# Attention probabilities read back from DRAM in four transfers by row block instead of four by partition block

## The chip, the cores and the metric

The kernel runs on one core of a Trainium2 chip. The metric is the device time of one execution in microseconds (us). The core has a matrix engine (TensorE, PE in the profile), a vector engine (VectorE, DVE), a scalar engine (ScalarE, ACT), GpSimd (POOL), and a sync engine (SyncE, SP), whose queue issues every transfer of this kernel. The transfers run on the core's 16 DMA engines.

## The reference

Eight batches of 112 tokens (width 1024) pass through two layers. Each layer has a cross attention against a context of 375 rows for each batch, and a low-rank mixture of experts. The change touches the second attention, which has 32 query heads in 8 groups of 4 (a group shares one key and one value head of width 128):

```python
q = apply_rope(query @ wq)          # 32 heads
k = apply_rope(key @ wk)            # 8 heads, each used by 4 query heads
scores = einsum('bhqd,bhkd->bhqk', q, k) / sqrt(128)
attn = softmax(scores + mask)
out = einsum('bhqk,bhkd->bhqd', attn, v)
return out.reshape(bs, sq, HQ * DV) @ wo
```

## The kernel before, in words

All arithmetic is float32. A product is made of three passes over operands split into a high and a low part: ScalarE rounds the high part, GpSimd or VectorE subtracts to get the low part.

The second attention is a pipeline of 64 steps, one for each pair of key group g and batch u (s = 8 g + u). `attention_phase` writes the order of each engine's queue out by hand. For one step s the work is: four score products (queries by keys, `scores`), mask and row minimum (`mask_scores`, L1696), exponentials (`exps`, L1704), normalisation, transposition of the probabilities, the product with the values (three key tiles, `o_banks`), and the projection with `wo` (`project`, 24 products a step).

The transposition is done in two parts. VectorE turns blocks of 32 by 32 inside groups of 32 partitions (`transpose`, L1739) and leaves them in `in_blocks[:, t]`, which has 128 partitions with 4 blocks of 384 numbers. Then the blocks must change partitions, and this goes through a DRAM tensor, `p_dram`, of shape (2, 128, 4, 384):

- `carry_out` (L1750) writes all of `in_blocks[:, t]` to `p_dram[t]` in one transfer of 768 KB.
- `carry_in` (L1761) waits until that transfer has landed (semaphore `carried`), and reads the data back into `pt_raw[t]` (the profile calls the two buffers `e_shuffled_then_xn_t` and `e_shuffled`) in four transfers of 192 KB. Row 32 i + a, block j of `p_dram[t]` goes to partition 32 j + a, place i. Every contiguous piece is 384 numbers, 1536 bytes, in both memories.

When all four have landed (semaphore `shuffled[t]` at a multiple of 64), ScalarE takes the high part of `pt_raw` (L1928), VectorE and GpSimd the low part (L1993, L1950), and TensorE multiplies with the values.

In step s the SP queue issues, in this order: `carry_out(s + 2)`, the queries and keys of step s + 6 (L1632, L1634), the values of step s + 2 (L1639), `carry_in(s + 2)`, and one or two tiles of `wo` (L1886). The queue is in order: while it waits in front of one transfer, the later ones are not issued. `carry_out(s + 2)` waits for the transposes of step s + 2, which VectorE does in step s. The second pair of these transposes comes behind VectorE's own part of the split of step s's probabilities (`probabilities_low(s)`), and so behind the landing of `carry_in(s)`. The carries of steps 0 and 1 are issued earlier, in `query1_phase`, between the last query projections.

Of the kernel before, what the change touches and what calls it, by code (L numbers as in the profile page):

```python
# [37 lines left out]
BLOCK, BLOCKS = 32, 4  # L38
# [1547 lines left out]
class AttentionSteps:  # L1586
# [165 lines left out]
    def carry_in(self, sp, s):  # L1752


        t = s % 2
        sp.wait_ge(self.carried, 16 * s + 16)
        if s >= 2:
            sp.wait_ge(self.pt_low_first, s - 1)
            sp.wait_ge(self.pt_low, 2 * s - 2)
        for j in range(BLOCKS):  # L1760
            sp.dma_start(self.pt_raw[t][BLOCK * j:BLOCK * (j + 1)],  # L1761
                         self.k.p_dram[t, :, j].rearrange("(i a) x -> a i x", i=BLOCKS)).then_inc(
                self.shuffled[t], 16)

    def load_mask(self, sp):
        sp.dma_start(self.mask, self.k.mask).then_inc(self.mask_in, 16)
# [676 lines left out]
```

## Time and profile before

| | us |
|---|---|
| median of 3 runs | 1777.59 |
| lowest, highest run | 1765.16, 1779.57 |
| the profiled execution: its own time | 1777.91 |
| the profiled execution: span, first to last instruction | 1776.1 |
| PE busy in the span | 1739.9 (98%) |
| transfers out to `p_dram`, x64, each | 768 KB, 6.4 from issue to landing |
| transfers back, x256, each | 192 KB, 3.8 or 3.9 from issue to landing |

The granted clock of TensorE was 1.00 for the core. A row of the profile's page is a share of the span or of one of 40 equal slices of it; the attention steps lie between 1137 and 1700 us.

### The profile page before, as it was taken

How to read it: one execution, taken by the hardware profiler on the slowest of the kernel's cores; microseconds unless marked ns; L12 is line 12 of the kernel's file. 1: busy time of each engine (PE TensorE's matmuls, PEld its weight loads, DVE VectorE, ACT ScalarE, POOL GpSimd, SP SyncE). 2: the span in 40 equal slices, each digit the busy share in tenths (PEclk: the TensorE clock that was granted, in tenths of full speed). 3: DMA queues.
4: the chain of work that ended last, by engine and by line, in shares of the span. 5: the costliest groups of instructions: out<-in, count | busy, mean ns of one | idle time of the engine just before them, and what ended most of it. 6: DMA issues, size and time to landing. Idle time of an engine off the chain costs nothing.

```text
span 1776.1 us, 26431 instructions
## 1 busy us (share of the span) xinstructions
PE 1739.9 (98%) x8904; PEld 1576.3 (89%) x8904; DVE 1102.9 (62%) x2116; ACT 735.6 (41%) x1532; POOL 783.0 (44%) x588
## 2 busy tenths in 40 slices
PE   7999999999999999999999999999999999999998
PEld 6999999999888888888999999889989999999876
DVE  7631275566433333336666668898888988888845
ACT  5211210012333233222111023487788888878724
POOL 3223522125422222201222234487777787777724
PEclk9999999999999999999999999999999999999999
DMA  4112342235643333423433335799999999899843
GB/s 135 66 51 83 133 132 85 84 104 162 206 128 121 114 111 117 127 82 99 127 108 89 111 108 163 203 291 265 263 286 278 286 264 276 268 274 278 243 134 111
DMA packets 186402, 291.55 MB, mean 164 GB/s; under 512 B 48336, under 2 KB 146896, under 8 KB 185280
## 3 DMA queue, kind: packets, MB, share of 16 engines
q1 hardware_dynamic: 186304, 290.33, 54.6%
q8 instruction: 51, 0.84, 0.2%
q14 instruction: 47, 0.39, 0.1%
HBM read 193.01 MB, written 97.26 MB: 163 GB/s over the span
## 4 chain that ended last, share of the span: by engine, by line
PE 56%; DMA 20%; SPq 6%; DVE 3%; issue 2%; ACT 1%; POOL 1%; DVEq 0%; ACTq 0%; POOLq 0%
PE bank L200 52%; DMA probabilities<-q_rotated_then_x_rows 17%; SPq L1761 4%; SPq L1886 1%; PE bank L106 1%; PE bank L2328 1%; PE bank L186 1%; PE bank L2341 1%; DVE e_scores L1696 1%; POOL shared_operand_low L324 1%; DMA aw_weights_then_ctx_rows<-in_wk 0%; DVE q_rotated_then_x_rows L1739 0%; DVE e_p_t_low L1993 0%; DMA e_raw_then_a<-q_rotated 0%; POOL w_rest_low L789 0%
## 5 line engine op out<-in xcount | busy, mean ns | idle before, releaser
L200 PE MATMUL bank<-shared_operand_high,w_first_high 128*128 128x448 f32 (+1 forms) x768 | 279.1, 363 | 1.6 <-DVEq L805 0.7
L200 PE MATMUL bank<-shared_operand_low,w_first_high 128*128 128x448 f32 (+1 forms) x768 | 278.4, 363 | 0.0
L200 PE MATMUL bank<-shared_operand_high,w_first_low 128*128 128x448 f32 (+1 forms) x768 | 278.3, 362 | 0.0
L324 POOL TENSOR_TENSOR shared_operand_low<-ctx_raw,shared_operand_high 128x768 fp32r<-128x768 f32 x64 | 119.4, 1877 | 197.4 <-ACT shared_operand_high L320 197.3
L1452 POOL TENSOR_TENSOR w_first_low<-aw_weights_then_ctx_rows,w_first_high 128x1024 fp32r<-128x1024 f32 x30 | 72.1, 2402 | 221.7 <-ACT w_first_high L1420 221.7
L1704 ACT ACTIVATE e_scores<-e_scores,e_least 128x375 f32<-128x375 f32 x256 | 152.5, 597 | 18.7 <-DVE e_least L1696 17.9
L200 PEld LDWEIGHTS bank<-shared_operand_high,w_first_high 128*128 128x128 f32 x768 | 144.7, 188 | 13.2 <-POOL w_first_low L496 1.0
L200 PEld LDWEIGHTS bank<-shared_operand_high,w_first_low 128*128 128x128 f32 x768 | 144.6, 188 | 11.4
L200 PEld LDWEIGHTS bank<-shared_operand_low,w_first_high 128*128 128x128 f32 x768 | 144.7, 188 | 11.1
L320 ACT ACTIVATE shared_operand_high<-ctx_raw 128x768 fp32r<-128x768 f32 x64 | 52.8, 843 | 209.4 <-DMA ctx_raw<-in_ctx_t 190.9
L1696 DVE CUSTOM_DVE_ANT_0 e_scores<-bank,e_mask_then_layer_ffn 128x375 f32<-128x375 f32 x256 | 134.6, 528 | 0.0
L1739 DVE STREAM_TRANSPOSE q_rotated_then_x_rows<-e_scores 128x768 f32<-128x768 f32 x128 | 124.2, 971 | 10.8 <-issue 8.4
L200 PE MATMUL bank<-shared_operand_high,w_rest_high 128*128 128x376 f32 x384 | 128.9, 336 | 1.6 <-POOL w_rest_low L789 1.6
L1420 ACT ACTIVATE w_first_high<-aw_weights_then_ctx_rows 128x1024 fp32r<-128x1024 f32 x30 | 31.8, 1061 | 236.8 <-PE bank L200 195.5
L200 PE MATMUL bank<-shared_operand_high,w_rest_low 128*128 128x376 f32 x384 | 128.6, 335 | 0.0
L200 PE MATMUL bank<-shared_operand_low,w_rest_high 128*128 128x376 f32 x384 | 128.6, 335 | 0.0
L200 PE MATMUL bank<-w_rest_high,shared_operand_high 128*128 128x512 f32 x288 | 112.9, 392 | 0.0
L200 PE MATMUL bank<-w_rest_high,shared_operand_low 128*128 128x512 f32 x288 | 112.4, 390 | 0.0
L200 PE MATMUL bank<-w_rest_low,shared_operand_high 128*128 128x512 f32 x288 | 112.2, 390 | 0.0
L1950 POOL TENSOR_TENSOR e_p_t_low<-e_shuffled_then_xn_t,e_p_t_high 128x448 fp32r<-128x448 f32 x64 | 83.1, 1321 | 56.2 <-ACT e_p_t_high L1928 56.2
L1950 POOL TENSOR_TENSOR e_p_t_low<-e_shuffled,e_p_t_high 128x448 fp32r<-128x448 f32 x64 | 83.1, 1318 | 52.5 <-ACT e_p_t_high L1928 52.5
L1717 DVE TENSOR_SCALAR e_scores<-e_scores,e_inv 128x375 f32<-128x375 f32 x128 | 99.7, 780 | 2.3
(259 smaller groups left out, 4542.8 us busy)
## 6 DMA issues: line engine op xcount, KB each, us to landing
probabilities<-q_rotated_then_x_rows SPq DMA_DIRECT2D x64, 768.0 KB, 6.4
ctx_raw<-in_ctx_t SPq DMA_DIRECT2D x64, 384.0 KB, 3.9
e_shuffled_then_xn_t<-probabilities SPq DMA_DIRECT2D x128, 192.0 KB, 3.8
e_shuffled<-probabilities SPq DMA_DIRECT2D x128, 192.0 KB, 3.9
e_raw_wo<-in_wo SPq DMA_DIRECT2D x64, 256.0 KB, 5.1
aw_weights_then_ctx_rows<-in_wq SPq DMA_DIRECT2D x30, 512.0 KB, 3.8
q_rotated<-q_rotated_then_x_rows SPq DMA_DIRECT2D x64, 224.0 KB, 2.3
e_raw_then_a<-q_rotated SPq DMA_DIRECT2D x64, 224.0 KB, 6.6
```

Source lines behind the costliest of these rows:

```text
L106: last = pe.transpose(banks[j][:, c * SEQ:(c + 1) * SEQ], buf.xn[:, k, ch * P:(ch + 1) * P], ident[0:SEQ, 0:SEQ])
L200: mm = pe.matmul(out, stationary[a], moving[b], start=(first and i == 0), stop=(last and i == 2))
L320: act.activation(k.ctx_ring[0][slot][:, 2 * j:2 * j + 2, :], k.c_raw[:, j % 2], ACT.Copy).then_inc(done, 1)
L324: pool.tensor_tensor(k.ctx_ring[1][slot][:, 2 * j:2 * j + 2, :], k.c_raw[:, j % 2], f32(k.ctx_ring[0][slot][:, 2 * j:2 * j + 2, :]), ALU.s ...
L1420: act.activation(k.w_first[0][:, t], k.raw[:, t], ACT.Copy).then_inc(w_high, 1)
L1452: pool.tensor_tensor(k.w_first[1][:, t], k.raw[:, t], f32(k.w_first[0][:, t]), ALU.subtract).then_inc(w_low, 1)
L1696: dve.tensor_tensor_reduce(self.s_buf[:, t, h, 0:KEYS], self.s_bank[h][:, 0:KEYS], self.mask[:, u, :], 1.0, HIGHEST, ALU.add, ALU.min, sel ...
L1704: act.activation(self.s_buf[:, t, h, 0:KEYS], self.s_buf[:, t, h, 0:KEYS], ACT.Exp, bias=self.least[:, t, h:h + 1], scale=-1.0, accum_out= ...
L1717: dve.tensor_scalar(self.s_buf[:, t, h, 0:KEYS], self.s_buf[:, t, h, 0:KEYS], self.inv[:, t, h:h + 1], None, ALU.mult).then_inc(self.norme ...
L1739: dve.transpose(self.in_blocks[:, t, :, h * piece:(h + 2) * piece].rearrange("p j (m k) -> p m j k", k=BLOCK), self.s_buf[:, t, h:h + 2, : ...
L1761: sp.dma_start(self.pt_raw[t][BLOCK * j:BLOCK * (j + 1)], self.k.p_dram[t, :, j].rearrange("(i a) x -> a i x", i=BLOCKS)).then_inc(self.sh ...
L1950: pool.tensor_tensor(by_block(pt[1][:, c, :]), raw_p(s, c), by_block(f32(pt[0][:, c, :])), ALU.subtract).then_inc(pt_low, 1)
```

## The change

The four transfers of `carry_in` are cut along the other axis. Before, transfer j filled the 32 partitions of block j with all four places i. After, transfer i fills place i of all 128 partitions. The number of transfers, the bytes of each, the 1536-byte pieces, the waits, the semaphores and the order on the queue are the same.

```diff
--- before.py
+++ after.py
@@ -1757,10 +1757,9 @@
         if s >= 2:
             sp.wait_ge(self.pt_low_first, s - 1)
             sp.wait_ge(self.pt_low, 2 * s - 2)
-        for j in range(BLOCKS):
-            sp.dma_start(self.pt_raw[t][BLOCK * j:BLOCK * (j + 1)],
-                         self.k.p_dram[t, :, j].rearrange("(i a) x -> a i x", i=BLOCKS)).then_inc(
-                self.shuffled[t], 16)
+        for i in range(BLOCKS):
+            sp.dma_start(self.pt_raw[t][:, i], self.k.p_dram[t, BLOCK * i:BLOCK * (i + 1)].rearrange(
+                "a j x -> j a x")).then_inc(self.shuffled[t], 16)
```

The access pattern of the source, from the slowest dimension to the fastest, was 32 rows, 4 places, 384 numbers; it becomes 4 blocks, 32 rows, 384 numbers. The destination was 32 partitions of 4 by 384 numbers; it becomes 128 partitions of 384 numbers.

## Rows read from the trace of the kernel before

**Rows 1.** The page: busy TensorE, and the span in 40 slices.
```profile
PE 1739.9 (98%) x8904; PEld 1576.3 (89%) x8904; DVE 1102.9 (62%) x2116; ACT 735.6 (41%) x1532; POOL 783.0 (44%) x588
...
PEclk9999999999999999999999999999999999999999
DMA  4112342235643333423433335799999999899843
GB/s 135 66 51 83 133 132 85 84 104 162 206 128 121 114 111 117 127 82 99 127 108 89 111 108 163 203 291 265 263 286 278 286 264 276 268 274 278 243 134 111
```

**Rows 2.** The chain that ended last, 1400 to 1480 us: shares by line.
```profile
by line: DMA probabilities<-q_rotated_then_x_rows 82.0%; SPq L1761 18.4%; SPq L1886 4.8%; issue 3.4%; SPq L1749 0.2%
```

**Rows 3.** Timeline of the SP queue, one step: start us, us, line, transfer, count.
```profile
1450.63 1.75 SPq L1761 DMA_DIRECT2D e_shuffled_then_xn_t<-probabilities  x4
1452.43 0.43 SPq L1886 DMA_DIRECT2D e_raw_wo<-in_wo  x1
1452.96 0.38 SPq L1750 DMA_DIRECT2D probabilities<-q_rotated_then_x_rows  x1
1453.38 0.43 SPq L1632 DMA_DIRECT2D e_raw_then_a<-q_rotated  x1
1453.85 1.40 SPq L1634 DMA_DIRECT2D e_raw_then_a<-k_rotated  x1
1455.30 0.80 SPq L1639 DMA_DIRECT2D e_raw_then_a<-v_rows  x1
1459.26 0.80 SPq L1761 DMA_DIRECT2D e_shuffled<-probabilities  x2
```

**Rows 4.** The same timeline: the transfers back of steps 0, 2 and 63.
```profile
1092.89 1.90 SPq L1761 DMA_DIRECT2D e_shuffled_then_xn_t<-probabilities  x4
...
1140.97 1.75 SPq L1761 DMA_DIRECT2D e_shuffled_then_xn_t<-probabilities  x4
...
1693.71 1.74 SPq L1761 DMA_DIRECT2D e_shuffled<-probabilities  x4
```

**Rows 5.** Stretches: from:to, length, busy by engine, TensorE clock, DMA share, GB/s.
```profile
1094.00:1099.00 5.00, 5.00 (x28) 4.79 (x27) 4.94 (x10) 0.00 (x0) 0.00 (x0) 1.00 0.99 254
...
1450.00:1453.00 3.00, 2.69 (x14) 2.21 (x13) 3.00 (x7) 2.66 (x9) 3.00 (x4) 1.00 0.64 182
1453.00:1456.00 3.00, 2.19 (x13) 1.87 (x11) 2.68 (x6) 3.00 (x8) 3.00 (x4) 1.00 1.00 213
1456.00:1459.00 3.00, 2.95 (x15) 2.74 (x16) 3.00 (x6) 2.37 (x7) 2.49 (x3) 1.00 1.01 382
...
1137.00:1700.00 563.00, 550.45 (x2781) 508.85 (x2781) 480.87 (x1046) 446.77 (x1098) 432.57 (x369) 1.00 0.92 272
1199.00:1699.00 500.00, 492.72 (x2494) 456.19 (x2493) 422.48 (x924) 396.88 (x977) 385.08 (x328) 1.00 0.91 270
...
1770.00:1776.00 6.00, 1.94 (x4) 0.63 (x4) 1.38 (x2) 0.08 (x1) 0.99 (x1) 0.90 0.47 153
```

**Rows 6.** The page's DMA issues: transfer, count, KB each, median us to landing.
```profile
probabilities<-q_rotated_then_x_rows SPq DMA_DIRECT2D x64, 768.0 KB, 6.4
...
e_shuffled_then_xn_t<-probabilities SPq DMA_DIRECT2D x128, 192.0 KB, 3.8
...
e_raw_wo<-in_wo SPq DMA_DIRECT2D x64, 256.0 KB, 5.1
...
e_raw_then_a<-q_rotated SPq DMA_DIRECT2D x64, 224.0 KB, 6.6
...
e_raw_then_a<-v_rows SPq DMA_DIRECT2D x64, 192.0 KB, 5.8
...
e_raw_then_a<-k_rotated SPq DMA_DIRECT2D x64, 188.0 KB, 6.7
```

## The prediction, made before the changed kernel was run

> **What bounds the kernel now.** I read the 40 slices of the page first. TensorE is busy for 98% of the span at full clock, and from slice 27 on, where the 64 attention steps lie, the 16 DMA engines are busy nine tenths of the time at 260 to 290 GB/s; before that they have room [rows 1]. So in the attention steps two resources are near their limit at once, and the change touches one of them. Next I read the chain that ended last, in a stretch of these steps: it does not run over TensorE at all. It is the transfer out, then the queue time of the four transfers back, then the `wo` load, and again the transfer out [rows 2]. The queue's timeline shows why: the four transfers back are issued at 1450.63, the next transfer out at 1452.96, and the queue then stands in front of the next transfers back until 1459.26, when that transfer out has landed [rows 3]. The transfer out takes 6.4 us [rows 6] because its packets stand behind those of the transfers back, which were issued just before. From the transfers back of step 2 (1140.97) to those of step 63 (1693.71) there are 61 steps, 552.74 us [rows 4], so one step is **9.06 us**. TensorE works 492.7 of 500 us there [rows 5], that is 8.93 us of each 9.06. The loop of transfers and TensorE are thus nearly equal: a shorter loop gains almost nothing, a longer one costs its whole length, 61 times.
>
> **The bytes of one step.** Out 768 KB, back 4 x 192 = 768 KB, queries 224, keys 188, values 192, `wo` 256 KB [rows 6]. With 1 KB = 1024 bytes the transfers back are 786 thousand bytes and all others 1628 KB, 1.667 million bytes. Spread over 16 engines this is 49.2 and 104.2 thousand bytes for each engine.
>
> **What a busy engine moves.** Divide the GB/s of a stretch by 16 and by the DMA share. Where the transfers back dominate (1453 to 1456) it is 213 / 16 / 1.00 = 13.3 GB/s; where the transfer out and the loads run (1456 to 1459) it is 382 / 16 / 1.01 = 23.6; around the transfers back of step 0 (1094 to 1099), with little else beside them, 254 / 16 / 0.99 = 16.0; over all steps 270 / 16 / 0.91 = 18.5 [rows 5]. The transfers back are the slow ones, though all engines are busy. They write into 32 partitions at a time, and the transfer out uses 128. That is the one thing in the rows that speaks for the change.
>
> **The change, part by part.** Nothing is removed: four issues a step before and after (1.75 us of queue time [rows 3], taken as unchanged), the same pieces and the same waits. What changes is how the pieces of one transfer are dealt out to the DMA engines. The source pattern had 32 entries in its slowest dimension and has 4 after. Transfers whose slowest dimension has 32 or 128 entries keep all 16 engines busy, since the share of the 16 reaches 0.99 to 1.01 in the stretches of both kinds [rows 5]. No transfer of the kernel before has a slowest dimension under 32, so no row prices this. The bounds are: dealt to all 16 engines as before, or dealt out by the slowest dimension, one of the four blocks j to one engine, with 12 engines left out. I take the second, because every other transfer of the kernel, seen from its code, can be divided over 16 engines by whole entries of its slowest dimension, and 4 entries can't.
>
> [...]
>
> If four engines carry everything, each of them gets 786 / 4 = 196.6 thousand bytes of the transfers back in a step, beside its 104.2 of the others, and these four set the time. One step then is a sum of three terms, because the transfer out of the next step stands behind the transfers back on the same engines, and the next transfers back are only issued when it has landed.
>
> - **The transfers back on one engine**: 196.6 / 23.6 = 8.3 us at the rate of the quick stretch, 196.6 / 13.3 = 14.8 us at the rate of the slow one. I take the rate around step 0's transfers back, 16.0, as it is the row with these very pieces and little else: **12.3 us**. Four engines alone may be quicker than sixteen that crowd on 32 partitions, which is why the quick end stays in the range.
> - **The other bytes of that engine**: 104.2 / 23.6 = 4.4 us to 104.2 / 18.5 = 5.6 us. The busy time of a step less that of the transfers back gives 0.91 x 9.06 - 49.2 / 13.3 = 4.5, or 5.2 with 16.0. I take **4.8 us**.
> - **The round trip that nothing covers**: between the landing of the transfer out and the first packets of the transfers back the engines run dry. In 1450 to 1453 the share is 0.64 [rows 5], so 0.36 x 3 = **1.1 us**. It could be 0 to 2.
>
> The sum is 18.2 us for a step; the ends are 4.4 + 8.3 + 1.1 = 13.8 and 5.6 + 14.8 + 1.1 = 21.5. Against 9.06 this is 9.14 x 61 = 558 us more. The last transfers back (issued at 1693.71) also land later by 12.3 - 49.2 / 16.0 = 9 us, and the product with the values waits for them. Those of steps 0 and 1 lie in a stretch where the queue and the engines have room, and they are needed only at the first steps; I cost them at nothing, at most 2 x 9 us if a weight load behind them comes late. TensorE's work of 8.93 us, and that of VectorE, ScalarE and GpSimd (480.9, 446.8 and 432.6 of 563 us [rows 5], so 7.7, 7.2 and 7.0 us a step) all fit below 18.2. The second pair of transposes, which the transfer out waits for, is done about 3 us after the previous landing, a time in which the four engines are busy with the next transfers back, so it adds nothing. What is late next is the split of the probabilities on ScalarE, GpSimd and VectorE, and TensorE behind them: it will stand idle for about half of each step.
>
> The profiled execution took 1777.91 us, 1.8 more than its span and 0.3 from the median of the three runs, so its sum holds for the median: 1777.9 + 558 + 9 = 2345 us. With the ends it is 1777.9 + 4.74 x 61 + 5 = 2072 and 1777.9 + 12.44 x 61 + 12 = 2549.
>
> **The rivals.**
> *All 16 engines, and quicker writes.* If the pieces are still dealt to 16 engines, each transfer now writes all 128 partitions. Then the 49.2 thousand bytes take 49.2 / 23.6 = 2.1 us and no longer 3.7, and 1.6 us a step leaves the loop. TensorE stands behind it at once: in the 563 us stretch it is idle for 12.6 us in all [rows 5], so the time is 1765 to 1778, say 1768. For it: the slow rate in 1453 to 1456. Against it: the four entries. This is the case on the other side, and it decides as soon as the transfer runs on all 16 engines.
> [...]
> *Four engines at the quick rate.* The rate of 23.6 holds with only four engines working: 13.8 us a step, 2072 us. For it: far less traffic at a time. Against it: the slow rows are of just these pieces.
> [...]
>
> **Chances.** Four engines with a step of 15.5 to 21 us (2170 to 2510): 0.66, and 2345 is its middle. Four engines at the quick rate (2050 to 2170): 0.20. All 16 engines: 0.10, of which half at no difference and a part faster. Slower than 2510, by waits that I don't see: 0.04. The range is 2050 to 2500; it leaves out the 16-engine case and the upper end, some 0.15. A measurement of this kernel can tell about 1%, 18 us, from no change: faster by more 0.03, within it 0.08, slower 0.89.
>
> **What would show each step.** In the changed kernel's slices DMA share would fall to about half or less (for the sum above: 300.8 thousand bytes on four engines, 104.2 on twelve, gives (4 x 17.1 + 12 x 4.8) / (16 x 18.2) = 0.43) at about 2.45 million bytes / 18.2 us = 135 GB/s. The transfers back would take over 10 us from issue to landing, the starts of L1761 would be 18 us apart, TensorE would be busy half the time in the steps, and its largest waits would be for the probabilities. If the share stays at nine tenths and the starts stay at 9 us, all 16 engines are used and the prediction is wrong in sign; if the starts are 14 us apart, only the rate was wrong.

## The result, and the profile after

The changed kernel takes 2134.32 us (median of 4 runs, 2130.72 to 2141.55) against 1774.92 before (median of 4 runs, the three of the table above and one more); the ratio of the means is **1.204**, with an interval of 1.1975 to 1.2102. The profiled execution took 2136.71 us, with a span of 2134.9. The forecast was 2345, with 2050 to 2500 as the range: the direction and the mechanism were right, the size was too large by 211 us, and the time lies in the case with the smaller chance (2050 to 2170, 0.20), not in the favoured one (2170 to 2510).

The page of the changed kernel, the lines that answer to [rows 1] with TensorE's busy share as well, then the packet counts, and those of the kernel before:

```profile
PE 1863.0 (87%) x8904; PEld 1657.0 (78%) x8904; DVE 1086.4 (51%) x2116; ACT 731.6 (34%) x1532; POOL 782.3 (37%) x588
...
PE   7999999999999999999998678777777777777678
...
PEclk9999999999999999999999888888888888888889
DMA  4123423463343323333455555555554555554443
GB/s 130 50 79 115 125 77 106 135 196 125 116 131 106 116 91 120 103 107 96 114 157 176 170 176 174 157 177 171 156 176 154 174 176 155 176 171 158 158 117 95
DMA packets 183330, 291.53 MB, mean 137 GB/s; under 512 B 45264, under 2 KB 143824, under 8 KB 182208
```

```profile
DMA packets 186402, 291.55 MB, mean 164 GB/s; under 512 B 48336, under 2 KB 146896, under 8 KB 185280
```

From slice 22 on everything is different: TensorE is no longer at 9, its mean clock is below full speed, and the DMA engines, which stood at nine tenths, stand at five tenths, though the loop that sets the step waits for transfers most of its time. I read that as a resource of which only a part is used, and the packets of the trace say which part. Before, there were 186402 packets; now there are 3072 fewer, all of them under 512 B, with the same pieces of data. They are packets of 4 bytes. The trace of the kernel before has 15088 of these, 16 for each of its 943 transfers, and 15088 updates of semaphores by transfers; that is why I call them completion packets. The trace of the changed kernel has 12016. The 687 other transfers, at 16 each as before, account for 10992, and 1024 are left for the 256 transfers back: 3072 / 256 = 12 fewer for each, 4 in place of 16. The updates of `shuffled` agree: 16 for each transfer back before (4096 in all), now 5 (1280), the first soon after the issue and four around the landing. That a completion packet stands for one engine at work on the transfer is my reading: with 16 of them to a transfer the DMA share reaches 0.99 to 1.01 [rows 5], and with 4 it is 0.25, as below.

The timeline of the SP queue: the transfers back of step 2; one step, to be read beside [rows 3] (the three loads behind the transfer out are left out here); the transfers back of step 63:

```profile
1146.65 2.37 SPq L1761 DMA_DIRECT2D e_shuffled_then_xn_t<-probabilities  x4
...
1500.26 2.46 SPq L1761 DMA_DIRECT2D e_shuffled_then_xn_t<-probabilities  x4
1502.76 0.79 SPq L1885 DMA_DIRECT2D e_raw_wo<-in_wo  x1
1503.65 0.38 SPq L1750 DMA_DIRECT2D probabilities<-q_rotated_then_x_rows  x1
...
1515.05 2.35 SPq L1761 DMA_DIRECT2D e_shuffled<-probabilities  x4
...
2042.34 2.40 SPq L1761 DMA_DIRECT2D e_shuffled<-probabilities  x4
```

The order is that of before, the distances are not: 11.4 us from the transfer out to the next transfers back, where there were 6.3. One step is (2042.34 - 1146.65) / 61 = **14.68 us**, against 9.06. The whole difference of 358.8 us between the two spans (2134.9 and 1776.1) splits into 5.7 us ahead of step 2's transfers back, 343.0 us in the 61 steps and 10.2 us behind them.

ScalarE in the same step, the first consumer of what comes back; in brackets its idle time before:

```profile
1512.52 1.51 ACT L1927 ACTIVATE e_p_t_high<-e_shuffled_then_xn_t 128x448 fp32r<-128x448 f32 x3 [7.12 <-DMA e_shuffled_then_xn_t<-probabilities]
```

The four transfers issued from 1500.26 on have landed at 1512.52, 12.3 us later; the page no longer gives a time to landing for them. The chain that ended last in 1400 to 1480 us, and stretches of the changed kernel (columns as in [rows 5]):

```profile
by line: DMA probabilities<-q_rotated_then_x_rows 84.2%; SPq L1761 15.7%; SPq L1885 5.8%; issue 1.9%; SPq L1749 0.1%
```

```profile
1503.00:1504.50 1.50, 1.50 (x7) 1.50 (x6) 0.80 (x3) 1.50 (x5) 1.50 (x2) 0.54 0.25 87
...
1137.00:2054.00 917.00, 678.35 (x2810) 592.70 (x2808) 468.85 (x1058) 446.65 (x1106) 435.79 (x371) 0.86 0.54 168
```

The chain is the loop of before, only longer. In 1503 to 1504.5 the DMA share is 0.25 at 87 GB/s, which is that of four engines always busy and twelve with nothing. The packets of the trace say the same of all 61 steps: in the third microsecond after the first of the four issues 3.9 packets are in flight on average, in the fourth 4.3. In the same 1.5 us the granted clock of TensorE is 0.54; the trace has only the levels 1.00 and 0.50, so it is nearly all of it at half speed.

The landings of the four transfers back can be read from the semaphore updates in the trace. Averaged over the 61 steps, they come 4.8, 7.2, 9.8 and 12.1 us after the first issue. So one transfer, 49.2 thousand bytes on each of the four engines, follows the other after 2.45 us, which is a rate of 20.0 GB/s for an engine, and the four take 9.8 us.

### The profile page after: what moved, and what is told of

Read it like the earlier page. It is cut to its first block, busy times and chain, and to the rows that moved or that the text cites. A ratio compares the mean times of both kernels' runs of the same rounds, so it can differ in the third digit from the quotient of the medians.

```text
span 2134.9 us, 26431 instructions
## 1 busy us (share of the span) xinstructions
PE 1863.0 (87%) x8904; PEld 1657.0 (78%) x8904; DVE 1086.4 (51%) x2116; ACT 731.6 (34%) x1532; POOL 782.3 (37%) x588
## 2 busy tenths in 40 slices
DMA packets 183330, 291.53 MB, mean 137 GB/s; under 512 B 45264, under 2 KB 143824, under 8 KB 182208
## 4 chain that ended last, share of the span: by engine, by line
PE 43%; DMA 34%; SPq 9%; DVE 2%; issue 2%; POOL 1%; ACT 1%; DVEq 0%; ACTq 0%; POOLq 0%
PE bank L200 39%; DMA probabilities<-q_rotated_then_x_rows 31%; SPq L1761 6%; SPq L1885 2%; DMA e_shuffled<-probabilities 1%; DMA aw_weights_then_ctx_rows<-in_wq 1%; PE bank L106 1%; PE bank L2327 1%; PE bank L186 1%; PE bank L2340 1%; DMA e_raw_wo<-in_wo 1%; POOL shared_operand_low L324 0%; DMA aw_weights_then_ctx_rows<-in_wk 0%; POOL w_rest_low L789 0%; PE bank L2310 0%
## 5 line engine op out<-in xcount | busy, mean ns | idle before, releaser
L200 PE MATMUL bank<-e_p_t_high,e_v_high 128*128 128x448 f32 x192 | 110.6, 576 | 225.8 <-DVE e_p_t_low L1992 222.9
L200 PEld LDWEIGHTS bank<-e_p_t_high,e_v_high 128*128 128x128 f32 x192 | 50.1, 261 | 271.5 <-issue 243.8
L324 POOL TENSOR_TENSOR shared_operand_low<-ctx_raw,shared_operand_high 128x768 fp32r<-128x768 f32 x64 | 119.0, 1872 | 196.6 <-ACT shared_operand_high L320 196.4
L1704 ACT ACTIVATE e_scores<-e_scores,e_least 128x375 f32<-128x375 f32 x256 | 151.8, 593 | 12.6 <-DVE e_least L1696 12.3
L1927 ACT ACTIVATE e_p_t_high<-e_shuffled 128x448 fp32r<-128x448 f32 x96 | 48.3, 566 | 212.3 <-DMA e_shuffled<-probabilities 212.3
L1927 ACT ACTIVATE e_p_t_high<-e_shuffled_then_xn_t 128x448 fp32r<-128x448 f32 x96 | 48.3, 566 | 206.9 <-DMA e_shuffled_then_xn_t<-probabilities 206.9
## 6 DMA issues: line engine op xcount, KB each, us to landing
e_raw_wo<-in_wo SPq DMA_DIRECT2D x64, 256.0 KB, 10.2
```

The lines of the kernel that those rows point to most:

```text
L200: mm = pe.matmul(out, stationary[a], moving[b], start=(first and i == 0), stop=(last and i == 2))
L324: pool.tensor_tensor(k.ctx_ring[1][slot][:, 2 * j:2 * j + 2, :], k.c_raw[:, j % 2], f32(k.ctx_ring[0][slot][:, 2 * j:2 * j + 2, :]), ALU.s ...
L1704: act.activation(self.s_buf[:, t, h, 0:KEYS], self.s_buf[:, t, h, 0:KEYS], ACT.Exp, bias=self.least[:, t, h:h + 1], scale=-1.0, accum_out= ...
L1927: act.activation(by_block(pt[0][:, c, :]), raw_p(s, c), ACT.Copy).then_inc(pt_high, 1)
```

## The experiments

Theory 1: the source of a new transfer has four entries in its slowest dimension, so it runs on four engines, and these set the step. Theory 2: all 16 engines work, but this cut is slow for each of them. Theory 3: a good part is TensorE's lower clock. Theory P, a guess from the 13.3 GB/s on 32 partitions against 23.6: some neighbouring blocks of 32 partitions slow each other when engines write both at once. The cuts of code leave out the counts of the waits on `shuffled`, which change with the number of transfers. Where nothing else is said, the edit is made to the changed kernel. Where a run is a single one, this is said; the kernel before, over all its runs, took 1758.89 to 1785.92 us, so a difference of some 20 us to a single run says nothing.

**One place of four by the new cut.** An edit to the kernel before:

```diff
+        sp.dma_start(self.pt_raw[t][:, 0], self.k.p_dram[t, 0:BLOCK].rearrange(
+            "a j x -> j a x")).then_inc(self.shuffled[t], 16)
         for j in range(BLOCKS):
-            sp.dma_start(self.pt_raw[t][BLOCK * j:BLOCK * (j + 1)],
-                         self.k.p_dram[t, :, j].rearrange("(i a) x -> a i x", i=BLOCKS)).then_inc(
+            sp.dma_start(self.pt_raw[t][BLOCK * j:BLOCK * (j + 1), 1:],
+                         self.k.p_dram[t, BLOCK:, j].rearrange("(i a) x -> a i x", i=BLOCKS - 1)).then_inc(
                 self.shuffled[t], 16)
```

> One of the four places by the new cut (one transfer of 192 KB), the other three by the old cut (four transfers of 144 KB). Theory 1 (a transfer whose source has 4 blocks in its slowest dimension runs on four engines, and these set the step): engines 0 to 3 carry 49.2 thousand bytes of the new kind, 36.9 of the old and 104.2 of the rest; a step is about 2.2 + 2.3 + 4.8 + 1.1 = 10.4 us, the time 1820 to 1900 us; the profile has 64 x 4 + 256 x 16 completion packets, so 186658 packets in all. Theory 2 (all 16 engines work, but filling one place in all 128 partitions is slow for each engine, in its writes or its reads of DRAM): a quarter of the extra 360 us as well, about 1865 us, but 64 x 16 completion packets, so 187426 in all.

Measured: 1905.26 us (4 runs; ratio to before 1.0755, interval 1.0697 to 1.0813), 186659 packets, of which 15344 have 4 bytes: 4 for each of the 64 new transfers and 16 for each of the 943 others. The count is that of theory 1 to within one packet and not theory 2's 187426. The time lies just above both theories' sums, so it decides nothing between them: a quarter of the new kind cost 133 us (against 1771.93, the median of the kernel before beside it), more than a quarter of 360. That the old kind's slow writes stay at the same time may be why; no run separates it.

**Pairs of blocks, two engines.**

```diff
         for i in range(BLOCKS):
-            sp.dma_start(self.pt_raw[t][:, i], self.k.p_dram[t, BLOCK * i:BLOCK * (i + 1)].rearrange(
-                "a j x -> j a x")).then_inc(self.shuffled[t], 16)
+            for n in range(0, BLOCKS, 2):
+                sp.dma_start(self.pt_raw[t][BLOCK * n:BLOCK * (n + 2), i],
+                             self.k.p_dram[t, BLOCK * i:BLOCK * (i + 1), n:n + 2].rearrange(
+                                 "a j x -> j a x")).then_inc(self.shuffled[t], 16)
```

> Each place in two transfers, blocks 0 and 1, then 2 and 3 (64 partitions, 96 KB each, 8 a step); the source has 2 entries in its slowest dimension. Theory 1: two engines carry all, 393 thousand bytes each in a step; a step is about 17.6 + 4.8 + 1.1 = 23.5 us, the time 2500 to 2850 us; DMA share in the steps falls to about 0.35. Theory 2: the same places in the same order on 16 engines, 2100 to 2200 us, DMA share as in the changed kernel.

Measured: 2619.28 us (one run). A stretch of its trace:

```profile
1200.00:1600.00 400.00, 199.69 (x810) 177.98 (x810) 136.59 (x308) 131.91 (x327) 130.44 (x111) 0.73 0.35 113
```

Half the engines for the same bytes in the same order cost 485 us more, at a DMA share of 0.35, as theory 1 had it. Theory 2 expected the share of the changed kernel and 2100 to 2200 us, and falls. From 2 to 11 us after the first issue of a step, 2.1 to 2.2 packets are in flight on average in each microsecond, where there were four. The trace has 12016 packets of 4 bytes: 687 x 16 and, for the 512 transfers back, 2 each.

**The same destination on 16 engines.** The DRAM tensor becomes (2, 4, 128, 384), so that the source of each transfer is 128 rows one after another; the turn from rows to blocks is done on the way out:

```diff
-        sp.dma_start(self.k.p_dram[t], self.in_blocks[:, t]).then_inc(self.carried, 16)
+        for i in range(BLOCKS):
+            sp.dma_start(self.k.p_dram[t, i].rearrange("(j a) x -> a j x", j=BLOCKS),
+                         self.in_blocks[BLOCK * i:BLOCK * (i + 1), t]).then_inc(self.carried, 16)
...
-        sp.wait_ge(self.carried, 16 * s + 16)
+        sp.wait_ge(self.carried, 64 * s + 64)
...
         for i in range(BLOCKS):
-            sp.dma_start(self.pt_raw[t][:, i], self.k.p_dram[t, BLOCK * i:BLOCK * (i + 1)].rearrange(
-                "a j x -> j a x")).then_inc(self.shuffled[t], 16)
+            sp.dma_start(self.pt_raw[t][:, i], self.k.p_dram[t, i]).then_inc(self.shuffled[t], 16)
```

> The destination is cut as in the changed kernel (place i of all 128 partitions), but the DRAM tensor is laid out by place, block and row, so that the source is 128 rows in order; for this the transfer out becomes four, one for each 32 partitions. Theory 1: 16 engines again; the transfers back become quick (about 2.1 us for an engine), the transfers out slow (1536-byte pieces out of 32 partitions, 3.1 to 3.7 us), and there are three more issues (1.3 us) in the loop: 1775 to 1870 us, 214050 packets. Theory 2: the writes are those of the changed kernel, so the time stays at 2100 us or more.

Measured: 1765.84 us (10 runs; ratio to before 0.998, interval 0.9955 to 1.0005), 214052 packets against 214050 expected; 18160 of them have 4 bytes, 16 for each of the 1135 transfers. The writes are those of the changed kernel, and its 360 us are gone. So the slow part was never the destination. That it was the four entries of the source, and not the order in which its rows lie in DRAM, which this run changes as well, is for the next run, which leaves that order as it is. The time came out 9 us below the range that I gave: the loop with four transfers out from 32 partitions each cost less than feared (8.86 us from the transfers back of one step to the next). The page, its chain over the whole span, and a stretch show what bounds it now:

```profile
DMA packets 214052, 291.58 MB, mean 165 GB/s; under 512 B 51408, under 2 KB 182736, under 8 KB 212928
...
PE 72%; DMA 7%; SPq 4%; DVE 3%; issue 2%; POOL 1%; ACT 1%; DVEq 0%; ACTq 0%; POOLq 0%
```

```profile
1200.00:1600.00 400.00, 399.46 (x2048) 375.16 (x2047) 345.46 (x772) 331.30 (x817) 321.16 (x274) 1.00 0.90 279
```

TensorE is busy for 399.46 of 400 us. The chain has left the transfers and lies on TensorE.

**Sixteen transfers of one block and place each.**

```diff
         for i in range(BLOCKS):
-            sp.dma_start(self.pt_raw[t][:, i], self.k.p_dram[t, BLOCK * i:BLOCK * (i + 1)].rearrange(
-                "a j x -> j a x")).then_inc(self.shuffled[t], 16)
+            for j in range(BLOCKS):
+                sp.dma_start(self.pt_raw[t][BLOCK * j:BLOCK * (j + 1), i],
+                             self.k.p_dram[t, BLOCK * i:BLOCK * (i + 1), j]).then_inc(self.shuffled[t], 16)
```

> The same places in the same order as the changed kernel, but each block by itself: 16 transfers of 48 KB, with 32 rows in the slowest dimension of both sides. Theory 1: 16 engines again (198690 packets); the queue's 16 issues of 0.43 us, 6.9 us a step, are the new cost: a step of 11.5 to 13 us, 1930 to 2030 us, DMA share 0.65 to 0.8. Theory 2: 2150 us or more, the slow writes and the issues together.

Measured: 2021.16 us (one run), 198696 packets. Places first, then blocks, as in the changed kernel, but on 16 engines: 113 us quicker than it, in spite of 12 more issues a step. The DRAM tensor and the 1536-byte pieces are those of the changed kernel. What differs is how many engines share a transfer, and how many partitions it fills, which the run before has ruled out. The count tells it once more: 1024 transfers of 16 packets in place of 256 of 4 are 15360 more, and the packets of 4 bytes are 15360 more (27376 against 12016; all packets together 15366). DMA share is 0.62 from 1200 to 1600 us, a little under the 0.65 that I expected. What bounds it is first of all the queue, by its chain in 1400 to 1480 us:

```profile
by line: SPq L1762 53.7%; DMA probabilities<-q_rotated_then_x_rows 39.9%; issue 6.5%; SPq L1886 3.7%; SPq L1749 0.1%
```

**TensorE lighter.** In `project`, one pass of three:

```diff
-                mm = split_product(pe, y_bank[t][:, 0:HALF],
-                                   [x[u % 4][:, h, t * P:(t + 1) * P] for x in wo],
-                                   [x[quad][:, h, :] for x in ot], h == 0, h == H - 1)
+                mm = pe.matmul(y_bank[t][:, 0:HALF], wo[0][u % 4][:, h, t * P:(t + 1) * P],
+                               ot[0][quad][:, h, :], start=h == 0, stop=h == H - 1)
```

> The changed kernel with one pass of three in the output projection: 8 products in place of 24 a step, so 16 x 0.2 = 3.2 us less TensorE work at full clock and up to 6.4 at half clock (the two passes with a low part are left out). Theory 1 (four DMA engines set the step): 2100 to 2145 us, and the starts of the transfers back stay 14.7 us apart. [...]

Measured: 2115.69 us (one run), 19 below the changed kernel. If TensorE's work set the step, 3.2 us less of it in each of 61 steps would be 195 us, and more at the lower clock.

```profile
1200.00:1600.00 400.00, 216.77 (x791) 190.46 (x792) 206.00 (x468) 200.27 (x498) 193.90 (x166) 0.74 0.54 169
```

TensorE works 217 us of these 400 in place of 297 and at a still lower mean clock (0.74 against 0.85), and DMA share and rate (0.54, 169 GB/s) are those of the changed kernel (0.54, 170). The transfers back of one step and the next lie 14.56 us apart, against 14.68. So neither TensorE's work nor the clock it is done at sets the step, and theory 3 falls. I take the lower clock for a consequence of the wait: TensorE does not stand in the chain of 1400 to 1480 us above at all, and in the same 400 us the mean clock is 1.00 where TensorE works 399 us (the run with rows in block order), 0.85 at 297 us, 0.74 at 217 and 0.73 at 200 (the pairs of blocks). What the clock costs by itself was not measured.

**Half the bytes back.**

```diff
-        for i in range(BLOCKS):
+        for i in range(BLOCKS if s < 2 else 2):
...
-                "a j x -> j a x")).then_inc(self.shuffled[t], 16)
+                "a j x -> j a x")).then_inc(self.shuffled[t], 16 if s < 2 else 32)
```

> The changed kernel with two of its four transfers back from step 2 on (places 0 and 1; places 2 and 3 keep the data of steps 0 and 1, so half of the reading back is left out). Theory 1: 98.3 thousand bytes less on each of the four engines; at 20 to 22 GB/s a step is 4.5 to 4.9 us shorter, at my 16.0 it would be 6.1; the time is 1835 to 1865 us (or 1760 at 16.0). The difference to the changed kernel, divided by 61, gives the rate. Theory 2 (all 16 engines, slow at this kind): half of the 786 thousand bytes less too, but with the old step's room the time falls to TensorE's floor, 1765 to 1800 us.

Measured: 1878.18 us (one run), 256 us below the changed kernel. That is 256.1 / 61 = 4.20 us a step for 98.3 thousand bytes on each of the four engines, a rate of **23.4 GB/s**. That is not the rate of the changed kernel, though. The saving is smaller than I expected (1878.18 us lies above the 1835 to 1865), and it gives a rate only if all the rest of a step goes as before. Here the second transfer back lands 3.4 us after the first, where it takes 2.5 us in the changed kernel, so the rest does not go as before. The two transfers that this run leaves out took 4.9 us there, from the second landing to the fourth. The packet count shows the four engines again: 124 transfers less are 16369 packets less (183330 against 166961), 132 for each: 128 pieces of 1536 bytes (25088 in the trace against 40960) and 4 packets of 4 bytes (11520 against 12016).

**A pair of blocks 32 partitions apart: blocks 0 and 1, then blocks 1 and 2.** The pair by the new kind of transfer, the other two blocks by the old kind. The edit is made to the kernel before; in the two kernels the numbers stand in place of `n` (0 in the first run, 1 in the second) and of `others`:

```diff
+        for i in range(BLOCKS):
+            rows = self.k.p_dram[t, BLOCK * i:BLOCK * (i + 1)]
+            sp.dma_start(self.pt_raw[t][BLOCK * n:BLOCK * (n + 2), i],
+                         rows[:, n:n + 2].rearrange("a j x -> j a x")).then_inc(self.shuffled[t], 16)
-        for j in range(BLOCKS):
+        for j in others:
             sp.dma_start(self.pt_raw[t][BLOCK * j:BLOCK * (j + 1)],
                          self.k.p_dram[t, :, j].rearrange("(i a) x -> a i x", i=BLOCKS)).then_inc(
                 self.shuffled[t], 16)
```

> Blocks 0 and 1 by the new kind of transfer (64 partitions, one place each, two entries in the source's slowest dimension), blocks 2 and 3 by the old kind. Theory 1 puts 196.6 thousand bytes of the pair, 24.6 of the others and 104.2 of the rest on engines 0 and 1: at about 20 GB/s for the pair a step is 9.8 + 1.5 + 4.8 + 0.5 = 16.6 us, 2240 us. [...] To be compared with the next run.

> The same with blocks 1 and 2 as the pair (partitions 32 to 95), and 0 and 3 by the old kind: the same bytes on the same engines. Without theory P the time is that of the run before within 30 us. [...]

Measured: 2223.25 us with blocks 0 and 1, 2206.12 us with blocks 1 and 2 (one run each), 184867 packets in both, 13552 of them of 4 bytes: 815 transfers at 16 and the 256 of the pair at 2. 17 us, 0.3 us a step, lies inside the 30 that I had called no difference. Both lie close to theory 1's 2240 us. At the 13.2 GB/s of 16 engines on 32 partitions the pair would take 196.6 / 13.2 = 14.9 us and not 9.8, 5.1 us more in each of 61 steps, some 310 us in all. So theory P, in the form that brings a pair down to that rate, falls: neither pair shows it.

**All four places in one transfer.** As the run with 16 engines and the new destination, but

```diff
-        for i in range(BLOCKS):
-            sp.dma_start(self.pt_raw[t][:, i], self.k.p_dram[t, i]).then_inc(self.shuffled[t], 16)
+        sp.dma_start(self.pt_raw[t], self.k.p_dram[t].rearrange("i p x -> p i x")).then_inc(self.shuffled[t], 16)
```

> As the run with the DRAM tensor laid out by place, block and row, but all four places come back in one transfer of 768 KB (128 partitions in the slowest dimension) with one issue. Theory 1: 16 engines; 210978 packets; three issues less in the loop. That loop no longer sets the step (TensorE works 99.9% of 1200 to 1600 us there), so the time stays at TensorE's floor: 1755 to 1775 us, within 0.5% of that run.

Measured: 1764.73 us (10 runs; ratio to before 0.994, interval 0.9914 to 0.9966), 210978 packets, as expected. TensorE is busy for 400.00 of the 400 us from 1200 on: nothing is left there that a change of the transfers could take away. These transfers back are also the quickest of all on 16 engines: in 1480.82 to 1482.02 us the core moves 385 GB/s at a DMA share of 1.02, which is 23.6 GB/s for an engine. In eleven steps from 1409 to 1500 us, over 1.2 us each, it is 18.5 to 23.6, with a median of 23.5.

**The kernel before, blocks in the order 0, 2, 1, 3.** An edit to the kernel before:

```diff
-        for j in range(BLOCKS):
+        for j in (0, 2, 1, 3):
```

> The kernel before with its four transfers back in the order of blocks 0, 2, 1, 3, so that neighbours in the queue write partitions 64 apart. [...]

Measured: 1765.43 us (10 runs; ratio to before 0.9926, interval 0.9897 to 0.9955).

```profile
1199.00:1699.00 500.00, 493.99 (x2513) 459.68 (x2513) 417.27 (x926) 399.57 (x975) 386.16 (x329) 1.00 0.88 273
```

DMA share falls from 0.91 [rows 5] to 0.88 while the GB/s rise from 270 to 273, so a busy engine moves a little more (19.4 against 18.5 GB/s). This fits a theory P for 16 engines that crowd on 32 partitions, but it rests on one profiled execution of each kernel. The gain in time is small, 0.7%: it is clear of its interval, but the median of the kernel before was itself 1771.93 us in one set of runs and 1779.25 in the set beside this one. So a weak form of theory P fits, and is not shown.

**What a busy engine moves, in three kernels.** The transfers back of step 0 have little beside them. The same stretches of the kernel before, of the run with rows in block order, and of the changed kernel:

```profile
1095.00:1096.00 1.00, 1.00 (x8) 1.00 (x7) 1.00 (x2) 0.00 (x0) 0.00 (x0) 1.00 1.07 226
1096.00:1097.00 1.00, 1.00 (x7) 0.99 (x6) 0.99 (x3) 0.00 (x0) 0.00 (x0) 1.00 1.07 226
```

```profile
1095.00:1096.00 1.00, 1.00 (x7) 0.97 (x6) 0.97 (x3) 0.00 (x0) 0.00 (x0) 1.00 0.94 292
1096.00:1097.00 1.00, 1.00 (x6) 0.93 (x6) 0.97 (x2) 0.00 (x0) 0.00 (x0) 1.00 0.95 295
```

```profile
1096.00:1097.00 1.00, 1.00 (x8) 0.95 (x7) 0.99 (x3) 0.00 (x0) 0.00 (x0) 1.00 0.26 97
```

GB/s divided by 16 and by the share gives 13.2 for 16 engines on 32 partitions, 19.4 for 16 engines on 128 partitions in four transfers, and 23.3 for four engines. The last is one microsecond of step 0; over a whole step of the changed kernel it is 20.0. The 16 engines of the run with all four places in one transfer reach about the same 23.5, so the number of engines at work alone does not make them slow; the 13.2 GB/s were found with the 32 partitions. A quarter of the engines at 20 to 23 is in any case far below all of them at 13.2.

## Why the prediction was right, and where its size was off

- **What bounds the kernel.** Right: two limits close together, the loop of transfers a hair longer than TensorE. With the loop relieved the kernel gained 0.2% to 0.7% and stopped at TensorE, and with the loop longer by 5.6 us a step it lost all of it, 61 times.
- **Four engines.** Right; no row of the kernel before showed such a transfer, and the four were an estimate from its patterns. The runs show it four ways: 12 completion packets fewer for each transfer back (15088 and 12016 of 4 bytes in all), a DMA share of 0.25 (four packets in flight) while the transfers back run alone, the time that comes back with 32 or 128 entries in the source's slowest dimension (2021.16 and 1765.84 us against 2134.32), and the 485 us that go with two entries. The count with two entries fits too: 512 transfers leave 2 x 512 completion packets, as many as 4 x 256, and the count is 183332 against 183330.
- **The sum.** The step was to be 18.2 us and is 14.68, and the mis-sized term is first of all the transfers back on one engine. I took 16.0 GB/s from the kernel's own rows of these pieces and got 12.3 us; the landings in the changed kernel give 20.0 GB/s and 9.8 us. That is 2.5 us too much in each of 61 steps, 152 us. The 16.0 was the rate of 16 engines that crowd on 32 partitions, and I carried it to four engines that don't. The quick-rate case, at 0.20, was the nearer one, and its 13.8 us a step missed the 14.68 by 0.9.
- **The other two terms** (4.8 and 1.1 us) were too large as well: 14.68 - 9.8 leaves 4.9 us for both, 1.0 us less, 63 us in all. The trace does not part them cleanly. With the 215 us off and 7 us on for the ends, the 2345 become 2137, and the profiled time is 2136.71.
- **The ends.** Steps 0 and 1, costed at nothing, cost 5.7 us; behind the last transfers back I expected 9 us, and it was 10.2.
- **The clock.** It fell, but only for a part of the time: TensorE worked 0.11 of the 3 us from 1510.5 to 1513.5, and from 1515 to 1516.5 its granted clock was 0.50; over the steps the mean is 0.86. At 0.50 all the time the 8.93 us of work would be 17.9, by my estimate, and the step longer than the 14.68 us that it is. TensorE was busy 678 of 917 us, 10.9 us of each 14.68, where I had it idle half the time, and the run with the lighter TensorE shows that this work did not set the step.
- **The profile after.** DMA share was to be 0.43 at 135 GB/s and is 0.54 at 168, both from the shorter step: 2.45 million bytes / 14.68 us = 167. The starts of L1761, 14.7 us apart, are the sign that I had named for "only the rate was wrong".
- **The range** held the time. Its lower end came from the quick rate; without that bound from the quick stretch the time would have been missed.

## What to carry to other kernels

Before a transfer is cut another way, write down the slowest dimension of both its sides. In the runs here a source with four entries there left the transfer to four engines (4 completion packets each, DMA share 0.25, 2134.32 us), though it filled 128 partitions, and one with two entries to two (2 packets each, 2619.28 us), though it filled 64; a destination with few entries was not tried. Where a transposition between partitions must go through DRAM, lay the DRAM tensor out so that each side starts with many entries, and put the short dimension in the middle: with 32 or 128 entries each transfer had 16 completion packets, and the kernels with one or four transfers back took 1764.73 to 1774.92 us. A low DMA share beside long waits for transfers was the sign of the fault (0.54 over the steps, 84.2% of the chain in the transfer out), and the number of packets told how many engines each transfer used.

## What the runs showed of the hardware

The rate of a busy DMA engine on the same 1536-byte pieces was 13.2 GB/s with 16 engines on 32 partitions, 19.4 with 16 engines on 128 partitions in four transfers, about 23.5 with the same in one transfer, and 20.0 over a whole step with four engines on 128 partitions. Two engines on blocks 0 and 1 and two on blocks 1 and 2, both pairs 32 partitions apart, differed by only 0.3 us a step, and with 16 engines on 32 partitions another order of the four transfers gained 0.7%, too little to be sure of. Of these kernels the rate was lowest in the one whose transfers of 192 KB wrote 32 partitions each, 13.2 against 19.4 and 23.5 GB/s on 128. But the runs with 19.4 and 23.5 also read their rows from DRAM in other orders, and no run here separates the two, so the cause stays open.
